# The third product of a two-element graph layer, by squared adjacency: seven block products with s3 held still

## The chip, the cores and the metric

The kernel runs on one core of a Trainium2 chip. The metric is the time of one execution on the device, in microseconds (us); the median of the runs counts. Five engines work side by side, each with its own queue in order: TensorE (PE; its weight loads PEld), VectorE (DVE), ScalarE (ACT), GpSimd (POOL) and SyncE (SP), which here only issues transfers. They wait for each other by semaphores that only count up.

## What is computed

Two graph networks follow one another, each with a residual and a layer norm. Only the first one, cut here, is touched by the change:

```python
def _slconv(x, adj, S, W):                       # S is adj: the weighting is adj squared
    support = jnp.einsum('bnf,fh->bnh', x, W)
    weighting = adj * S
    return jnp.einsum('nm,bmh->bnh', weighting, support)
h = jax.nn.relu(_slconv(x, adj, S, W1))          # W1 128 x 256
h = jax.nn.relu(_slconv(h, adj, S, W2))          # W2 256 x 512
return _slconv(h, adj, S, W3)                    # W3 512 x 128
...
x = _layernorm(x + _L0_gnn_ref(x, adj, adj, W1, W2, W3), axis=-1)   # x (8, 1024, 128), adj 1024 x 1024
x = _layernorm(x + _L1_gnn_ref(x, adj, ...), axis=-1)               # graph layers and four LSTMs
```

The third product of this text is the last one with the squared adjacency, adj^2 times s3, where s3 = h W3 is 1024 x 128 for each of the eight elements.

## The kernel before

Every float32 factor is kept as two parts, a high part that TensorE reads as it is and a low part that is the rest, so a product is three matmuls: high by high, high by low, low by high. ScalarE makes the high part (L1422, a copy with rounding), VectorE the low part (L1672, source less high part).

The eight elements go through the first network in **four pairs** ("pair" and `it`; elements 0 and 1 of a pair). Pair 0 is written out, pairs 1 and 2 are one loop body, the last pair is written out again. Then come the second network and its LSTMs in slots, which the change leaves as they are.

Products with the squared adjacency come in two forms. The products with x and with h1 use Strassen's scheme in Winograd's form: adj and the other factor are cut in 2 x 2 blocks of 512, and **seven block products** P1, P5, P6, P3, P7, P2, P4 take the place of eight. Each (`block_product`, L848) is twelve matmuls: four tiles of 128 columns of a block B held still, 512 columns of a block of adj or of its sums `sx` moving. The right-hand blocks are B11, B21, B22 and the differences T1 to T4; T1 = (B12's block, kept at T3) - B11, T2 = B22 - T1, T3 = B12 - B22, T4 = B21 - T2. Each is made as raw data (a copy from PSUM by ScalarE, or a subtraction by VectorE, L1822), then split. The results are added up by VectorE over q, r and the "C sums" (L1851, L1858, L1867).

The **third product** is done plainly. s3 of an element comes out of TensorE transposed (features on the partitions, `s3_product`). VectorE copies it to `s3t` (L1885), TensorE turns each half back by four transposes (`turn_half`, L1022), ScalarE and VectorE split it to `s3`. Then for each of eight rows of tiles m, four units u and two tiles t, a tile of adj is held still and 256 columns (both elements side by side) of s3 move: `a3_tile`, L1030, 8 x 4 x 2 x 3 = 192 matmuls of 256 columns. The result lies already as x does; VectorE adds it to x (`pair_sums`, L2063 and L2070), takes row statistics and, somewhat later, norms the rows.

While this runs, the next pair is made ready: GpSimd forms the differences of its x blocks (`x_diffs`, L794 to L799, four subtractions), ScalarE and VectorE split them as "n B11" to "n T4" to `t7`.

The order on each engine is written out by hand. The tables `MM_...`, `HI_...` and `LO_...` list the names that TensorE, ScalarE and VectorE signal, in order; a wait for a name is a wait for its place in the table. `BANK_OF` gives each result one of the eight PSUM banks. x is loaded to `xp` a first time for the differences and a second time, after "n T4", for the sums.

Of the kernel before, what the change touches and what calls it, by code (L numbers as in the profile page):

```python
# [38 lines left out]
def build(nc, x, adj_t, w1, w2, w3, wg0, bg0, wg1, bg1, wih_t, whh_t, bih, bhh, xn, out):  # L39
# [12 lines left out]
    with ctx:  # L52
# [46 lines left out]
        from_a11 = sb("from_a11", [P, 2, BANK], F32, s3t_at)  # L99
        tile_sum = sb("tile_sum", [P, N], F32, s3t_at + 4 * N)  # L100
# [138 lines left out]
        def w1_names(e, u0, u1):  # L239
# [3 lines left out]
        MM_TAIL = (h2_names(0, 0, 0, K3) + h2_names(0, 1, 0, 2) + ["0 s3 0"] + h2_names(0, 1, 2, K3)  # L243
                   + w1_names(1, 0, 2) + ["0 s3 1"] + w1_names(1, 2, 4)
                   + seven(1) + h2_names(1, 0, 0, K3) + h2_names(1, 1, 0, 2) + ["1 s3 0"] + h2_names(1, 1, 2, K3)
                   + ["turn 0 0", "turn 1 0", "1 s3 1", "turn 0 1", "turn 1 1", "a3 first"]
                   + [f"a3 {u}" for u in range(A3)])
        PLAIN = ["0 C11", "0 C12", "0 C21", "0 C22"]
        MM_FIRST = ["x0 0", "x0 1", "x1 0", "x1 1"] + w1_names(0, 0, 4) + PLAIN + MM_TAIL
        MM_NEXT = (["x P1", "x P5", "x P6", "x P3", "x P7", "x P2"] + w1_names(0, 0, 2) + ["x P4"]  # L250
                   + w1_names(0, 2, 4) + seven(0) + MM_TAIL)

# [4 lines left out]
        def hi_second(e, *names):  # L257
# [5 lines left out]
        HI_ONE = (["1 raw 0", "1 raw 1", "1 B11", "1 T1", "1 raw 2", "1 raw 3", "1 T2", "1 B22", "1 p1", "1 T4",  # L263
                   "1 T3", "1 B21"] + hi_second(1, *C_ORDER) + ["s3 0 0", "s3 1 0", "s3 0 1", "s3 1 1"])
        HI_X = ["n B11", "n B22", "n B21", "n T1", "n T2", "n T3", "n T4"]
        FROM_A11 = ["from a11 0", "from a11 1"]
        HI_TAIL = HI_ONE + HI_X + FROM_A11
# [5 lines left out]
        HI_LAST = HI_START + hi_second(0, *C_ORDER) + HI_ONE + ["n x"] + FROM_A11  # L273
# [4 lines left out]
        def lo_second(e, *names):  # L278
# [4 lines left out]
                   "1 T3", "1 B21", "1 T4", "1 r"] + lo_second(1, *LO_C) + ["s3 0 0", "s3 1 0", "1 s3t 1", "s3 0 1", "s3 1 1"])  # L283
        LO_X = ["n B11", "n B22", "n B21", "n T1", "n T2", "n T3", "n T4"]
        X_DIFFS = ("T1", "T2", "T3", "T4")
        LO_TAIL = LO_ONE + LO_X
# [5 lines left out]
        LO_START = SUMS + ["x q", "x r", "x C12 sum", "x C12", "x C22 sum", "x C22", "x C11", "0 T1 sum", "0 B11",  # L292
# [53 lines left out]
        def adj_part(i, m, cols):  # L346
            if cols is square_tile:
# [13 lines left out]

        def bank(name):
            return ps[:, BANK_OF[name], :]


        def c_block(e, name, part):

            n = {"C11": (0, 0), "C12": (1, 0), "C21": (0, 1), "C22": (1, 1)}[name]
            cols = slice(n[1] * BANK, (n[1] + 1) * BANK)
# [4 lines left out]
            return y2_raw[:, n[0], cols] if part == "raw" else y2[:, part, n[0], cols]  # L374

# [445 lines left out]
        def _(pe):  # L821
# [20 lines left out]
            B_BLOCK = {1: B11, 2: B21, 3: B22, 4: T4, 5: T1, 6: T2, 7: T3}  # L842

            def block_product(dst, v, start):
                for t in range(QUARTER):
                    tile = slice(t * P, (t + 1) * P)
                    for a, b in ((HI, HI), (HI, LO), (LO, HI)):
                        last = pe.matmul(dst, t7[:, B_BLOCK[v], a, tile], A_BLOCK[v](b, t),  # L848
# [85 lines left out]
            def pair_products(it):  # L934
                first = isinstance(it, int) and it == 0
# [49 lines left out]
                def adjacency(e):  # L985

                    lo_done(f"{e} B11")
                    signals(block_product(bank(f"{e} a"), 1, True), f"{e} P1")
                    lo_done(f"{e} T1")
                    signals(block_product(bank(f"{e} e"), 5, True), f"{e} P5")  # L990
                    lo_done(f"{e} T2")
                    signals(block_product(bank(f"{e} b"), 6, True), f"{e} P6")
                    lo_done(f"{e} B22")
                    signals(block_product(bank(f"{e} c"), 3, True), f"{e} P3")
                    lo_done(f"{e} r", f"{e} T3")
                    signals(block_product(bank(f"{e} b"), 7, False), f"{e} P7")
                    lo_done(f"{e} B21")
                    hi_done(f"{e} p1")
                    signals(block_product(bank(f"{e} a"), 2, False), f"{e} P2")
                    lo_done(f"{e} T4", f"{e} C22 sum")  # L1000
                    signals(block_product(bank(f"{e} b"), 4, False), f"{e} P4")
# [9 lines left out]
                def s3_product(e, half):  # L1011
# [4 lines left out]
                    signals(last, f"{e} s3 {half}")  # L1016

# [66 lines left out]
                turn_half(0, 0)  # L1084
                turn_half(1, 0)
                s3_product(1, 1)
                turn_half(0, 1)

                lo_done("s3 0 0", "s3 1 0")
                for m in range(MT):  # L1090
                    if m == 1:
                        turn_half(1, 1)
                    if m == QUARTER:
                        lo_done("s3 0 1", "s3 1 1")
                    for u in (2, 3, 0, 1) if m == QUARTER else range(A3):
                        if m == QUARTER and u < 2:
                            hi_done(f"from a11 {u}")
                        for t in range(2):
                            last = a3_tile(m, u, t)
# [1244 lines left out]
```

## Time and profile before

| | us |
|---|---|
| median of 3 runs | 983.54 |
| lowest, highest | 983.18, 983.77 |
| the profiled execution: its own time | 983.22 |
| its span on the core, in the profile | 981.5 |
| TensorE busy in the span | 966.2 (98%) |
| VectorE, ScalarE, GpSimd busy | 650.9, 429.9, 35.2 |
| one pair, start of the third product to the next one's | 120.42 |

The page of the profile gives, in this order, the busy time of each engine, the span in slices, the transfers, the chain of work that ended last and the costliest groups of instructions. Times of single rows are counted from the start of the span. The recorded time of a matmul runs to the end of its result, beyond the start of the next one; what a row of matmuls costs is the step from start to start. The same holds for VectorE and ScalarE, whose instructions overlap a little.

### The profile page before, as it was taken

To read this page: it belongs to the slowest core of one execution; us is meant where nothing else is said; L and a number is where in the kernel's file an instruction comes from. 1 tells how busy PE (TensorE), PEld (TensorE's weight loads), DVE (VectorE), ACT (ScalarE), POOL (GpSimd) and SP (SyncE) were. 2 spreads that over 40 slices of the span, in tenths; PEclk is the share of its full clock that TensorE was granted. 3 is DMA by queue.
4 is the path that set the end of the run, shared out by engine and by line. 5 is a ranking of instruction groups with operands and counts; after the bars stand their busy time and mean duration, and the time that the engine had idled before them with its cause. 6 is when DMAs were issued, how large, how long until landed. Compare 5 with 4: busy or idle time off the path is not lost.

```text
span 981.5 us, 14408 instructions
## 1 busy us (share of the span) xinstructions
PE 966.2 (98%) x5279; PEld 846.3 (86%) x5279; DVE 650.9 (66%) x1442; ACT 429.9 (44%) x788; POOL 35.2 (4%) x34
## 2 busy tenths in 40 slices
PE   9999999999999999999999999999999999999994
PEld 7888998889888898888988898898988889898894
DVE  7765557454575545754766656877776786877987
ACT  6353403433044331352434445455454555455765
POOL 0000200002000020000000001001010000100000
PEclk9999999999999999999999999999999999999998
DMA  8000000101011010104600000000000000000001
GB/s 306 1 1 1 13 32 18 69 1 44 0 43 43 0 43 1 61 26 143 232 2 0 1 1 1 0 2 22 1 1 22 0 22 0 22 1 22 1 1 65
DMA packets 11287, 31.01 MB, mean 32 GB/s; under 512 B 1120, under 2 KB 2400, under 8 KB 11232
## 3 DMA queue, kind: packets, MB, share of 16 engines
q1 hardware_dynamic: 11232, 30.30, 8.4%
q8 instruction: 32, 0.52, 0.2%
q14 instruction: 23, 0.19, 0.1%
HBM read 22.95 MB, written 7.34 MB: 31 GB/s over the span
## 4 chain that ended last, share of the span: by engine, by line
PE 95%; DVE 3%; ACT 1%; issue 1%; DVEq 0%; ACTq 0%
PE ps L1192 24%; PE ps L848 19%; PE ps L824 11%; PE ps L826 11%; PE ps L825 11%; PE ps L1030 9%; PE ps L1245 3%; PE ps L1265 2%; PE ps L866 2%; PE ps L1113 1%; PE ps L1022 1%; PE ps L1307 1%; DVE stats L1689 1%; PE ps L1339 1%; PE ps L1308 0%
## 5 line engine op out<-in xcount | busy, mean ns | idle before, releaser
L848 PE MATMUL ps<-adj,t 128*128 128x512 f32 x480 | 112.9, 390 | 0.0
L848 PEld LDWEIGHTS ps<-adj,t 128*128 128x128 f32 x480 | 89.3, 188 | 18.0
L1030 PE MATMUL ps<-s,adj 128*128 128x256 f32 x768 | 94.1, 284 | 0.0
L1030 PEld LDWEIGHTS ps<-s,adj 128*128 128x128 f32 x768 | 92.6, 192 | 0.0
L824 PE MATMUL ps<-adj,node 128*128 128x512 f32 x216 | 84.5, 391 | 0.1
L826 PE MATMUL ps<-adj,node 128*128 128x512 f32 x216 | 84.3, 390 | 0.0
L825 PE MATMUL ps<-adj,node 128*128 128x512 f32 x216 | 84.3, 390 | 0.0
L1610 ACT ACTIVATE gates_x<-ps,lb 128x258 f32<-128x258 f32 (+1 forms) x156 | 66.5, 508 | 40.3 <-PE ps L1192 40.2
L1610 ACT ACTIVATE gates<-ps,lb 128x512 f32<-128x512 f32 (+2 forms) x117 | 66.7, 647 | 37.9 <-PE ps L1192 28.7
L848 PE MATMUL ps<-sx,t 128*128 128x512 f32 x360 | 83.2, 389 | 0.0
L848 PEld LDWEIGHTS ps<-sx,t 128*128 128x128 f32 x360 | 67.6, 188 | 14.0
L1675 DVE SCALAR_TENSOR_TENSOR h<-ps,h 128x512 fp32r<-128x512 f32 x80 | 54.4, 688 | 37.2 <-ACT h L1422 37.2
L1192 PE MATMUL ps<-hw,lw 128*128 128x258 f32 (+1 forms) x468 | 72.4, 303 | 0.0
L1192 PEld LDWEIGHTS ps<-hw,lw 128*128 128x128 f32 x468 | 68.5, 190 | 2.3
L1422 ACT ACTIVATE y<-y_raw 128x512 fp32r<-128x512 f32 x27 | 17.1, 632 | 116.2 <-DVE y_raw L1867 116.2
L1422 ACT ACTIVATE h<-ps 128x512 fp32r<-128x512 f32 x64 | 38.1, 598 | 60.2 <-PE ps L826 60.2
L1192 PE MATMUL ps<-hstep_x,lw 128*128 128x258 f32 (+1 forms) x360 | 53.7, 298 | 0.0
L1192 PEld LDWEIGHTS ps<-hstep_x,lw 128*128 128x128 f32 x360 | 50.8, 189 | 0.4
L826 PE MATMUL ps<-y,w2s 128*128 128x512 f32 x128 | 49.8, 389 | 0.0
L824 PE MATMUL ps<-y,w2s 128*128 128x512 f32 x128 | 49.8, 389 | 0.0
L825 PE MATMUL ps<-y,w2s 128*128 128x512 f32 x128 | 49.8, 389 | 0.0
L826 PEld LDWEIGHTS ps<-adj,node 128*128 128x128 f32 x216 | 40.6, 188 | 8.5
(250 smaller groups left out, 1819.2 us busy)
## 6 DMA issues: line engine op xcount, KB each, us to landing
xb<-in_x SPq DMA_DIRECT2D x7, 1024.0 KB, 4.9
sx_raw<-in_adj_t SPq DMA_DIRECT2D x8, 512.0 KB, 8.6
adj_raw<-in_adj_t SPq DMA_DIRECT2D x8, 512.0 KB, 7.8
out<-xb SPq DMA_DIRECT2D x7, 512.0 KB, 2.6
xn<-xb SPq DMA_DIRECT2D x3, 1024.0 KB, 4.0
xb<-xn SPq DMA_DIRECT2D x6, 512.0 KB, 6.9
xb<-in_x SPq DMA_DIRECT2D x2, 512.0 KB, 5.4
lw_raw<-in_wih_t SPq DMA_DIRECT2D x1, 1024.0 KB, 11.3
```

Source lines behind the costliest of these rows:

```text
L824: pe.matmul(dst, stat(HI), mov(HI), start=start, stop=False)
L825: pe.matmul(dst, stat(HI), mov(LO), start=False, stop=False)
L826: return pe.matmul(dst, stat(LO), mov(HI), start=False, stop=stop)
L848: last = pe.matmul(dst, t7[:, B_BLOCK[v], a, tile], A_BLOCK[v](b, t), start=start and t == 0 and (a, b) == (HI, HI), stop=t == QUARTER - 1 ...
L866: pe.matmul(bank(f"{name} {half}"), of[:, a, m * P:(m + 1) * P], adj[:, b, m, half * BANK:(half + 1) * BANK], start=(m == 0 and (a, b) == ...
L1030: last = pe.matmul(dst, adj[:, a, m, nt:nt + P], s3[:, b, m, :, :].rearrange("p j c -> p (j c)"), start=(m == 0 and t == 0 and (a, b) == ( ...
L1192: done = pe.matmul(gate_bank(a), lw[:, i, weight, names[a] * F:(names[a] + 1) * F], state(j), start=start and (i, j) == (HI, HI), stop=sto ...
L1245: last = pe.matmul(mm_unit("adj_x", half), node[:, i, m * P:(m + 1) * P], adj[:, j, m, half * BANK:(half + 1) * BANK], start=(m == 0 and ( ...
L1265: last = pe.matmul(mm_unit("wg0", v)[:, t * F:(t + 1) * F], z[:, i, nt:nt + P], wgs[:, j, 0, :], start=(t == 0 and (i, j) == (HI, HI)), st ...
L1422: nc.scalar.activation(dst, src, func).then_inc(a_hi, 1)
L1610: nc.scalar.activation(gates_in(u.stream)[:, g, at], ps[:, (AHEAD["gate"][slot] + gate) % GB, 0:u.n], ACT.Tanh if g == GG else ACT.Sigmoid ...
L1675: nc.vector.scalar_tensor_tensor(out=dst, in0=src, scalar=0.0, in1=f32(hi), op0=ALU.max, op1=ALU.subtract).then_inc(done, 1)
```

## The change

In pairs 0, 1 and 2 the third product is done by seven block products as well; the last pair keeps the plain form.

- s3t of the two elements is turned back by `flip_half` (as `turn_half`, other banks): element 0's halves after the third block product of h1 of element 1 ("flip 0 0", "flip 0 1"), element 1's first half before "1 s3 1", its second half after P1 of the new stage. ScalarE copies each from PSUM as raw data (`flip_raw`); element 1 gives B11 and B21, element 0 gives B12 (at T3) and B22.
- The stage "s": T1 to T4 and the splits as in the other seven-block products, in tiles `s7_...` of their own laid over `node`, the place of y1, y2 and s3, and the end of the big buffer; then P1 (flip 1 1 behind it), P5, P6, P3, P7, P2, P4.
- The result is transposed (features on the partitions). Three of its blocks, C12, C22 and C11, are turned back at the end of the stage (`back_block`, 12 transposes), C21 after the first block product of the next pair (4 more). VectorE adds the four to x in four passes of 512 columns in place of six.
- The differences of the next x by GpSimd stay where they were, behind "1 s3 1"; "n B11" to "n T4" and r, the C sums of "s" are woven into one another on VectorE.

```diff
+        S3_AT = {"B22": node_at, "T3": node_at + 4 * KB, "B11": r2_at, "T1": r2_at + 4 * KB, "T2": r2_at + 8 * KB,
+                 "B21": r2_at + 12 * KB, "T4": big_at + 28 * KB}
...
+        MM_H2 = h2_names(1, 0, 0, K3) + h2_names(1, 1, 0, 2) + ["1 s3 0"] + h2_names(1, 1, 2, K3)
+        MM_TAIL = (MM_MIDDLE + seven(1)[:3] + ["flip 0 0", "flip 0 1"] + seven(1)[3:] + MM_H2
+                   + ["flip 1 0", "1 s3 1", "s P1", "flip 1 1"] + seven("s")[1:] + ["back C12", "back C22", "back C11"])
...
+        HI_TAIL = (HI_H1 + ["s raw 0 0", "s raw 0 1", "s B22"] + hi_second(1, *C_ORDER)
+                   + ["s raw 1 0", "s B11", "s T1", "s T2", "s T3", "s raw 1 1", "s p1", "s B21", "s T4", "n B11",
+                      "n B22", "n B21", "n T1", "n T2", "n T3", "n T4", "s C11"])
...
+        LO_TAIL = LO_ONE + ["s T1 sum", "s B11", "1 s3t 1", "s T2 sum", "s T1", "s T3 sum", "s B22", "s T4 sum", "s T2",
+                            "s T3", "s B21", "s q", "s T4", "n B11", "s r", "n B22", "n B21", "n T1", "n T2", "n T3",
+                            "n T4", "s C12 sum", "s C22 sum", "s C21 sum"]
...
+                def transposed(dst, src):
+                    for t in range(4):
+                        last = pe.transpose(dst[:, t * F:(t + 1) * F], src[:, t * P:(t + 1) * P], ident_f[:])
+                    return last
...
+                    pe.wait_ge(a_lo, reached_before("lo", it, "s C21 sum"))
+                    back_block("C21")
                     signals(block_product(bank("x e"), 5, True), "x P5")
...
+                else:
+                    flip_half(1, 0)
+                    s3_product(1, 1)
+                    adjacency("s")
+                    lo_done("s C12 sum")
+                    back_block("C12")
+                    lo_done("s C22 sum")
+                    back_block("C22")
+                    hi_done("s C11")
+                    back_block("C11")
...
+                    for name in BACK:
...
+                        nc.vector.tensor_tensor(rows, rows, bank(f"back {name}"), ALU.add).then_inc(a_lo, 1)
+                    own_done("sum C21")
                     row_stats(pair_rows(), stats_at(it - 1))
```

TensorE at the third product of pair 0, before (the twelve products on `h2` and `w3s` between the first two rows are left out):

```order
L1022 MATMUL ps<-ident_f_98,s3t_67 128x128 x4
L1030 MATMUL ps<-s3_63,adj_49 128x256 x24
L1022 MATMUL ps<-ident_f_98,s3t_67 128x128 x4
L1030 MATMUL ps<-s3_63,adj_49 128x256 x168
L1120 UNCONDITIONAL_BRANCH
```

and now:

```order
L874 MATMUL ps<-adj_49,s7_B11_73 128x512 x12
L1051 MATMUL ps<-ident_f_113,s3t_67 128x128 x4
L874 MATMUL ps<-sx_89,s7_T1_74 128x512 x12
L874 MATMUL ps<-sx_89,s7_T2_75 128x512 x12
L874 MATMUL ps<-sx_89,s7_B22_71 128x512 x12
L874 MATMUL ps<-adj_49,s7_T3_72 128x512 x12
L874 MATMUL ps<-adj_49,s7_B21_76 128x512 x12
L874 MATMUL ps<-adj_49,s7_T4_77 128x512 x12
L1051 MATMUL ps<-ident_f_113,a3_out_70 128x128 x12
```

The 192 products on adj held still have gone, and 84 of 512 columns with s3's blocks held still, then twelve transposes, stand there.

VectorE from the last two low parts of h2 of pair 0 on, before:

```order
L1675 SCALAR_TENSOR_TENSOR h2_54<-ps,h2_54 128x512 x2
L1672 TENSOR_TENSOR s3_63<-ps,s3_63 128x4x128 x2
L1885 COPY s3t_67<-ps 128x512
L1672 TENSOR_TENSOR s3_63<-ps,s3_63 128x4x128 x2
L1672 TENSOR_TENSOR t7_52<-xb_76,t7_52 128x512 x3
L1672 TENSOR_TENSOR t7_52<-t7_raw_53,t7_52 128x512 x4
```

and now:

```order
L1752 SCALAR_TENSOR_TENSOR h2_54<-ps,h2_54 128x512 x2
L1897 TENSOR_TENSOR s7_T1_raw_81<-s7_T3_raw_79,s7_B11_raw_80 128x512
L1749 TENSOR_TENSOR s7_B11_73<-s7_B11_raw_80,s7_B11_73 128x512
L1962 COPY s3t_67<-ps 128x512
L1897 TENSOR_TENSOR s7_T2_raw_82<-s7_B22_raw_78,s7_T1_raw_81 128x512
L1749 TENSOR_TENSOR s7_T1_74<-s7_T1_raw_81,s7_T1_74 128x512
L1897 TENSOR_TENSOR s7_T3_raw_79<-s7_T3_raw_79,s7_B22_raw_78 128x512
L1749 TENSOR_TENSOR s7_B22_71<-s7_B22_raw_78,s7_B22_71 128x512
L1897 TENSOR_TENSOR s7_T4_raw_84<-s7_B21_raw_83,s7_T2_raw_82 128x512
L1749 TENSOR_TENSOR s7_T2_75<-s7_T2_raw_82,s7_T2_75 128x512
```

Behind the copy of "1 s3 1" there stood one more split of s3 and then the next x; now there stand the differences and low parts of s3's blocks, each with two inputs in SBUF.

## Rows read from the trace of the kernel before

**Rows 1.** The page: busy time of the engines, and the chain by engine.

```profile
PE 966.2 (98%) x5279; PEld 846.3 (86%) x5279; DVE 650.9 (66%) x1442; ACT 429.9 (44%) x788; POOL 35.2 (4%) x34
...
PE 95%; DVE 3%; ACT 1%; issue 1%; DVEq 0%; ACTq 0%
```

**Rows 2.** Busy time by window; PEclk is the granted clock, last two are transfers.

```profile
core 0: us, PE busy (x) PEld busy (x) DVE busy (x) ACT busy (x) POOL busy (x), PEclk, DMA share, GB/s
110.87:231.29 120.42, 120.42 (x655) 104.77 (x654) 69.12 (x161) 38.59 (x66) 5.14 (x5) 1.00 0.08 27
...
106.90:134.41 27.51, 27.51 (x221) 26.98 (x220) 14.17 (x34) 7.50 (x14) 5.08 (x4) 1.00 0.12 39
```

**Rows 3.** Timeline of TensorE, pair 0 to 1: start, length, line, operation, count.

```profile
106.90 1.03 PE L1022 MATMUL ps<-ident_f,s3t 128*128 128x128 f32 x8
107.69 0.48 PE L824 MATMUL ps<-h,w3s 128*128 128x512 f32 x1
...
110.51 0.60 PE L1022 MATMUL ps<-ident_f,s3t 128*128 128x128 f32 x4
...
114.17 20.40 PE L1030 MATMUL ps<-s,adj 128*128 128x256 f32 x168
134.41 2.91 PE L848 MATMUL ps<-adj,t 128*128 128x512 f32 x12
137.16 8.32 PE L848 MATMUL ps<-sx,t 128*128 128x512 f32 x36
145.32 5.60 PE L848 MATMUL ps<-adj,t 128*128 128x512 f32 x24
150.76 0.28 PE L824 MATMUL ps<-w1s,y 128*128 128x256 f32 x1
```

**Rows 4.** Timeline of TensorE, transposes among 512-column products, in the later phase.

```profile
618.08 0.60 PE L1339 MATMUL ps<-ident_f,hfull 128*128 128x128 f32 x4
618.44 3.03 PE L1192 MATMUL ps<-hstep,lw 128*128 128x512 f32 x12
```

**Rows 5.** Timeline of ScalarE and VectorE at the third product of pair 0.

```profile
107.09 0.60 ACT L1422 ACTIVATE h<-ps 128x512 fp32r<-128x512 f32 x1 [0.77 <-PE ps L826]
...
107.72 0.69 DVE L1675 SCALAR_TENSOR_TENSOR h<-ps,h 128x512 fp32r<-128x512 f32 x1 [0.67 <-ACT h L1422]
...
110.71 0.69 DVE L1885 COPY s3t<-ps 128x512 f32<-128x512 f32 x1 [1.10 <-PE ps L826]
...
117.66 2.48 DVE L1672 TENSOR_TENSOR t<-t_raw,t 128x512 fp32r<-128x512 f32 x4
```

**Rows 6.** Timeline of GpSimd and of VectorE where they meet, pair 0.

```profile
110.83 1.29 POOL L794 TENSOR_TENSOR t_raw<-xb 128x512 f32<-128x512 f32 x1 [109.45 <-PE ps L826]
...
114.69 1.29 POOL L799 TENSOR_TENSOR t_raw<-xb,t_raw 128x512 f32<-128x512 f32 x1
...
115.70 0.83 DVE L1672 TENSOR_TENSOR t<-xb,t 128x512 fp32r<-128x512 f32 x1
```

**Rows 7.** Timeline of VectorE and of GpSimd near the end of the kernel.

```profile
914.89 0.72 DVE L2156 TENSOR_TENSOR gates_x<-gates_x 128x258 f32<-128x258 f32 x1
915.54 1.11 DVE L2158 TENSOR_TENSOR gates_x<-gates_x 128x258 f32<-128x258 f32 x1
916.68 0.43 DVE L2161 TENSOR_TENSOR gates_x<-gates_x 128x258 f32<-128x258 f32 x1
...
915.28 1.08 POOL L816 CAST hw_last<-ht_last 128x516 fp32r<-128x516 f32 x1
```

**Rows 8.** Timeline of TensorE, a restart after a wait for ScalarE.

```profile
958.72 0.96 PE L1317 MATMUL ps<-lw,wgs 128*128 128x512 f32 x3 [0.88 <-ACT gates_last L1610]
```

**Rows 9.** Timeline of VectorE: constants after pair 0, and the low part of C22.

```profile
120.09 0.06 DVE L2081 MEMSET sel<- 128x4 f32 x1
...
122.90 0.17 DVE L2100 MEMSET ones<- 128x128 f32 x1
...
149.62 0.69 DVE L1672 TENSOR_TENSOR y<-y_raw,y 128x512 fp32r<-128x512 f32 x1 [0.70 <-ACT y L1422]
```

More of the change, by code:

```diff
@@ L291, in build @@
         SUMS = ["sum a11 2", "sum a11 3", "sum 0", "sum 1", "sum 2", "sum 3"]
-        LO_START = SUMS + ["x q", "x r", "x C12 sum", "x C12", "x C22 sum", "x C22", "x C11", "0 T1 sum", "0 B11",
+        BACK = ("C12", "C22", "C11", "C21")
+        LO_START = [f"sum {name}" for name in BACK] + ["x q", "x r", "x C12 sum", "x C12", "x C22 sum", "x C22", "x C11", "0 T1 sum", "0 B11",
                            "x C21 sum", "0 T2 sum", "0 T1", "0 T4 sum", "0 T2", "0 T3 sum", "0 B22", "x C21", "0 q",
@@ L374, in c_block, with seven_block @@
             return y2_raw[:, n[0], cols] if part == "raw" else y2[:, part, n[0], cols]
+        BLOCK = {"B11": B11, "T1": T1, "T2": T2, "B22": B22, "T3": T3, "B21": B21, "T4": T4}
+        def seven_block(e, name, part):
+            if e == "s":
+                return s7_raw[name][:] if part == "raw" else s7[name][:, part, :]
+            return t7_raw[:, BLOCK[name], LO, :] if part == "raw" else t7[:, BLOCK[name], part, :]
         PLAIN_AT = {"C11": "a", "C12": "b", "C21": "e", "C22": "c"}
@@ L841, in _, with block_product @@
                        3: lambda i, t: sx[:, S4, i, t, :]}
-            B_BLOCK = {1: B11, 2: B21, 3: B22, 4: T4, 5: T1, 6: T2, 7: T3}
-            def block_product(dst, v, start):
+            B_BLOCK = {1: "B11", 2: "B21", 3: "B22", 4: "T4", 5: "T1", 6: "T2", 7: "T3"}
+            def block_product(dst, v, start, e=None):
                 for t in range(QUARTER):
@@ L1083, in pair_products @@
                 h2_product(1, 1, 3)
[L1084 to L1099, printed above, removed]
[L1100 to L1105 removed]
+                if last_pair:
+                    turn_half(0, 0)
+                    turn_half(1, 0)
+                    s3_product(1, 1)
+                    turn_half(0, 1)
+                    lo_done("s3 0 0", "s3 1 0")
+                    for m in range(MT):
+                        if m == 1:
+                            turn_half(1, 1)
+                        if m == QUARTER:
+                            lo_done("s3 0 1", "s3 1 1")
+                        for u in (2, 3, 0, 1) if m == QUARTER else range(A3):
+                            if m == QUARTER and u < 2:
+                                hi_done(f"from a11 {u}")
+                            for t in range(2):
+                                last = a3_tile(m, u, t)
+                            if (m, u) == (QUARTER - 1, 1):
+                                signals(last, "a3 first")
+                            if m == MT - 1:
+                                signals(last, f"a3 {u}")
+                        if m < MT - 1:
+                            last.then_inc(adj_used, 1)
+                else:
+                    flip_half(1, 0)
+                    s3_product(1, 1)
+                    adjacency("s")
[5 more added lines that the diff above has]
+                    back_block("C11")
@@ L1468, in turned_hi, with flip_raw @@
                           bank(f"turn {e} {half}").rearrange("p (t c) -> p t c", t=4), ACT.Copy)
+                def flip_raw(e, half):
+                    mm_done(f"flip {e} {half}")
+                    to = {(0, 0): "T3", (0, 1): "B22", (1, 0): "B11", (1, 1): "B21"}[e, half]
+                    hi_of(f"s raw {e} {half}", seven_block("s", to, "raw"), bank(f"flip {e} {half}"), ACT.Copy)
                 def x_hi_of(name):
@@ L1550, in pair @@
                 block_hi(1, "B21")
+                if not last_pair:
+                    flip_raw(0, 0)
+                    flip_raw(0, 1)
+                    block_hi("s", "B22")
                 c_hi(1, "C12")
@@ L1570, in pair @@
                         block_hi("n", name)
-                if last_pair:
+                    mm_done("s P2")
+                    hi_of("s C11", c_block("s", "C11", "raw"), bank("s a"), ACT.Copy)
+                else:
+                    turned_hi(0, 0)
+                    turned_hi(1, 0)
+                    turned_hi(0, 1)
+                    turned_hi(1, 1)
                     act.wait_ge(xb_in, 16 * (B - 2))
@@ L1575, in pair @@
                     tile_hi(1)
-                for u in range(2):
-                    mm_done("a3 first")
-                    hi_of(f"from a11 {u}", from_a11[:, u, :], bank(f"a3 {u}"), ACT.Copy)
+                    for u in range(2):
+                        mm_done("a3 first")
+                        hi_of(f"from a11 {u}", from_a11[:, u, :], bank(f"a3 {u}"), ACT.Copy)
                 assert n_hi[0] == len(names)
```

171 lines of the change are left out of this document (102 added, 69 removed), and 2 rows, old and new, of the table BANK_OF.

## The prediction, on record before the changed kernel was timed

> **What bounds the kernel now.** I read the page's shares first: TensorE is busy in 98% of the span and the chain that ended last lies on it for 95% [rows 1]. So a microsecond taken off TensorE's queue is one microsecond of time, as long as nobody makes TensorE wait. The table by windows then gives the frame of the phase that is changed: one pair takes 120.42 us, TensorE is busy in all of it, and the granted clock is 1.00 [rows 2]. The changed stretch of a pair goes from the first transpose of the third layer to the next pair's first block product, 106.90 to 134.41, 27.51 us, with VectorE at half load and GpSimd busy for 5.08 us in it [rows 2, 3]. This is why the second thing to read is who else could become late: today the others have slack here, and the change takes it away.
>
> **TensorE, what goes.** In those 27.51 us lie the twelve s3 products, which are unchanged. Their step is that of every 512-column product: 36 of them from 137.16 to 145.32, so 226.7 ns each, 2.72 us for twelve [rows 3]. The rest, 27.51 - 2.72 = 24.79 us, is the 192 products of 256 columns and four groups of transposes (8, 4 and 4 instructions in three places). For the big part of it: 168 products in 114.17 to 134.41, 120.5 ns each, against 226.7 ns for twice the columns. So a 256-column product costs more than half of a 512-column one, and the old stage is 192 such.
>
> **What comes.** Seven block products of twelve, 84 x 226.7 ns = 19.04 us; same form of stationary and moving operand as the ones timed. Then 32 transposes instead of 16. Among 512-column products a transpose costs more than its own step: eight start at 106.90 and the next product at 107.69, and from there to the transpose at 110.51 twelve products take 2.82 instead of 2.72, so eight cost 0.79 + 0.10 = 0.89 [rows 3]. Four: 618.08 to 618.44 is 0.36; the next twelve products end after 3.03, where 11 steps and a last one of 0.39 (the 36 above take 8.32, 0.16 beyond their steps) are 2.88, so 0.51 in all [rows 4]; as eight lose only 0.10 behind them, I take 0.49. Twelve, at 0.11 each from the same rows: 1.36. The change has groups of 8, 4, 4, 12 and 4: 0.89 + 3 x 0.49 + 1.36 = 3.72 us. TensorE's work thus goes from 24.79 to 19.04 + 3.72 = 22.76: **2.03 us less per pair**, 6.1 us in three pairs. Bounds: 2.7 if a group costs only its 0.09 to 0.11 steps, 1.7 if every group costs 0.1 more. The last pair keeps the old form and the phase after the pairs is untouched.
>
> **Who makes TensorE wait.** Now every block product needs a B block or a difference of B blocks, each split in a high part (ScalarE) and a low part (VectorE), all made from s3 while the stage is already running. I walk it in the clock of pair 0, 0.89 later than before since eight transposes now stand in the product before. Durations and hand-over: a ScalarE pass over 512 columns 0.60, a VectorE one 0.69, or 0.60 for each more in a row; a pass starts 0.03 after what it waits for (107.69 to 107.72) [rows 5].
> P1 could start at 111.00: flip at 107.79, 0.49, 2.72. B11: raw copy to 109.08, high to 109.71, low to 110.42. In time by 0.6.
> P5 could start at 111.00 + 2.72 + 0.49 = 114.21 and needs T1's low part, P6 2.72 later and needs T2's. VectorE cannot begin these before it has copied "1 s3 1" (result there at 111.16, copy 111.19 to 111.88), because its queue is in order. Undisturbed: T2 sum to 112.5, T1 low to 113.1, T3 sum to 113.7, B22 low to 114.3, T4 sum after the copy of flip 1 1 by ScalarE at about 115.0, so to 115.7, T2 low to 116.3. P5 and P6 would be in time by 1.1 and 0.6 us, and the whole 2.03 us would stay.
>
> **The disturbance.** GpSimd makes its four differences of x, 1.29 us each, exactly then: it waits for the same "1 s3 1" as VectorE's copy and starts right behind it, 110.83 after 110.71 [rows 5, 6]. Before, VectorE had at that time a copy from PSUM, 0.69 long with GpSimd running beside it [rows 5], and little else. The one VectorE pass with two SBUF inputs that still met GpSimd's last difference is the one at 115.70: 0.83 instead of 0.68, ended at 116.53, 0.55 after GpSimd's 115.98 [rows 6]. So it did not run beside it: it waited until 0.13 before GpSimd's end and then took its 0.68. And in 914.89 to 916.65 the two take turns: a VectorE product ends at 915.61, the next was issued at 915.54 right behind it but takes 1.11 us where the following one takes 0.43, because a GpSimd cast, issued at 915.28 and ended at 916.36, came in between; again VectorE ends 0.29 after it, 0.14 before and 0.43 of its own [rows 7].
> The Trainium skill says the same: "SBUF — State Buffer", section "Who interferes with whom", has a VectorE instruction with two SBUF inputs and a GpSimd instruction that reads SBUF exclude each other, the later one to issue blocked until the other is done; by that rule, which the rows above bear out, the stage is paced by both engines together and not by the slower one.
> T2 sum, T1 low, T3 sum, B22 low, T4 sum and T2 low all have two SBUF inputs. Taking turns: GpSimd 1 starts some 0.1 behind the copy, 111.26 to 112.55; T2 sum ends 112.55 + 0.55 = 113.10. GpSimd 2 gets in just before that (I take the same 0.12 the other way round), ends 114.27; T1 low ends 114.82. GpSimd 3 to 115.99; T3 sum ends 116.54. GpSimd 4 to 117.71; B22 low ends 118.26, T4 sum 118.86, T2 low 119.46. ScalarE's copy of flip 1 1 stands behind T3's high part in its queue (117.2) and is there at 117.8, just before T4 sum wants it. A restart costs TensorE the hand-over and an exposed weight load: three products took 0.96 after a wait, where 2 x 0.227 + 0.39 is 0.84, so 0.12 [rows 8]. P5 starts at 114.82 + 0.15 = 114.97 instead of 114.21, wait 0.76; P6 could start at 117.69 and starts at 119.61, wait 1.92. **2.68 us of waits per pair.** From there VectorE is free of GpSimd and catches up: r is ready at about 123.2 and P7 starts at 125.05; the sum that P4 needs is there about 1.5 us before it.
>
> **The start of the next pair.** The four sums, the row statistics and q, r come about as late against the block products as before, so pairs 2 and 3 wait for nothing. In pair 1 VectorE's constants (120.09 to 123.07), which lay in idle time, now lie between the last sum of pair 0 and the first of pair 1. Low C22, ended at 150.31 for a product at 150.76 before [rows 9], has by the same walk between 0 and 0.2 left: I put 0.1 us, once.
>
> **Sum.** 3 x (2.68 - 2.03) + 0.1 = +2.05 us. Against the profiled execution: span 981.5 to 983.6. It lies 1.7 us of start and end below its own time of 983.22, which is 0.3 below the median 983.54; the difference is put on the median: 983.54 + 2.05 = **985.6 us**. The likeliest case's own range is 983.8 to 987.6: 0.35 us per pair either way on the transposes and 0.5 on the waits.
>
> **Rivals.**
> (a) VectorE keeps its turn. If a waiting GpSimd gets in only where VectorE's queue has a gap, T1 low ends at 113.7 and P5 is in time; the gap comes at 115, before T4 sum, and T2 low ends at 117.2: wait 0.5 us per pair. 3 x (0.5 - 2.03) + 0.1 = -4.5: 979.0 us. This is the case on the other side. It speaks for it that VectorE's passes stand back to back here; against it the turn at 915.54, where a pass issued right behind the last one was overtaken [rows 7]. It decides at one row: the second and third GpSimd difference of the stage longer than 1.29 us by several VectorE passes.
> (b) No exclusion at all: no wait, 3 x -2.03 + 0.1 = -6.0: 977.5. Against it stands the 0.83 [rows 6].
> (c) The turns hold but one of the two waits is smaller, since GpSimd starts later or T1 low slips in before its second: 1 us less per pair, 982.6.
> (d) Worse: ScalarE's copy of flip 1 1 comes late for T4 sum (it has some 0.4 us), or T2 low loses one more turn: 1 us more per pair, 988.6.
> That the products of the stage are not as fast as the others' is the rival in which the change does not do what it says; nothing in the profile speaks for it, and it is in the bounds above.
>
> **Chances.** Likeliest case 0.68, (a) 0.10, (b) 0.05, (c) 0.08, (d) 0.09. A measurement of this kernel can tell about 0.2%, 1.97 us, from no change: under 981.6 is faster, over 985.5 slower. The likeliest case lies on that border: I give 0.36 of its 0.68 to slower and 0.32 to the same; with (d) slower is 0.44, with half of (c) the same is 0.36, and faster is (a), (b), the other half of (c) and a rest: 0.20. The range goes from (a) to nearly (d): 978.8 to 988.5, and leaves out (b), part of (a) and part of (d), some 0.15.
>
> **What the profile after would show.** Products on blocks of s3: step 0.227 us. A group of four transposes among them: under 0.5 us. TensorE idle before the weight load of the second and the third product of the stage, released by VectorE's low part of T1 and of T2, about 0.8 and 1.9 us, in all three pairs, and nowhere else. VectorE's differences and low parts there about 1.3 us long beside GpSimd and 0.68 after it; GpSimd's four differences stretched over 6.5 us instead of 5.15. Pair to pair 121.1 us instead of 120.4. The forecast is wrong if TensorE has no idle time there (b), if GpSimd is stretched to much over 7 us (a), or if TensorE waits at a third place, above all P7 for r.

## The result, and the profile after

The changed kernel takes **985.38 us** (median; 984.93 to 985.97), the kernel before 983.25 us in the same comparison (983.1 to 983.77). The ratio is 1.0021, with a 95% interval of 1.0012 to 1.003: slower by 2.13 us, where +2.05 was forecast. The profiled execution's own time is 984.93 us, its span 983.1, so the two traces that are compared here lie 1.6 to 1.7 us apart.

The page of the kernel after, busy time by engine and the chain by engine; the rows before are [rows 1]:

```profile
PE 961.5 (98%) x5003; PEld 828.1 (84%) x5003; DVE 679.4 (69%) x1472; ACT 442.8 (45%) x809; POOL 38.9 (4%) x34
...
PE 92%; DVE 5%; issue 1%; ACT 1%; DVEq 0%; ACTq 0%
```

TensorE has less to do (961.5 instead of 966.2 us busy), and yet the kernel is longer. VectorE's share of the chain has gone from 3% to 5%: work of VectorE now stands between two products. GpSimd's busy time has grown from 35.2 to 38.9 us although its 34 instructions are the old ones. Which VectorE work that is, the table of TensorE's waits tells (line waited at, releaser, then total us, times, longest). In the kernel before no line of that table named a block of s3:

```profile
PEld ps L874 <- DVE s_T L1749: 8.4, 6, 2.0
```

Six waits, two in each of three pairs. The timeline of TensorE in pair 0 of the kernel after shows where they lie; these rows answer to [rows 3] (start, length, line, form, count, and in brackets the idle time before it and who ended it):

```profile
110.35 2.88 PE L874 MATMUL ps<-adj,s_B 128*128 128x512 f32 x12
113.07 0.60 PE L1051 MATMUL ps<-ident_f,s3t 128*128 128x128 f32 x4
114.26 3.01 PE L874 MATMUL ps<-sx,s_T 128*128 128x512 f32 x12 [0.59 <-DVE s_T L1749]
118.86 3.06 PE L874 MATMUL ps<-sx,s_T 128*128 128x512 f32 x12 [1.59 <-DVE s_T L1749]
121.75 2.88 PE L874 MATMUL ps<-sx,s_B 128*128 128x512 f32 x12
124.47 2.88 PE L874 MATMUL ps<-adj,s_T 128*128 128x512 f32 x12
...
132.64 1.47 PE L1051 MATMUL ps<-ident_f,a_out 128*128 128x128 f32 x12
133.87 3.02 PE L874 MATMUL ps<-adj,t 128*128 128x512 f32 x12
```

The two rows of `sx,s_T` are P5 and P6, on T1 and T2 of s3. From the starts: with the flip at its 0.49, P5 could have come at 110.35 + 2.72 + 0.49 = 113.56 and comes at 114.26, 0.70 late; P6 could have come at 114.26 + 2.72 = 116.98 and comes at 118.86, 1.88 late, and the product behind it comes after 2.89 instead of 2.72, 0.17 for the restart. From there on the steps are 2.72. From the first column of P1 to the transposes back is 132.64 - 110.35 = 22.29 us: seven times 2.72, 0.49 for the flip, and 2.76 for the waits (0.70 + 1.88 + 0.17, rounded). Pairs 1 and 2 read the same way with slightly smaller waits: P5 starts 0.62 late, P6 1.89 late, and the restart costs 0.13, in all 2.64 and 2.65 us.

VectorE and then GpSimd at the same place (GpSimd's rows answer to [rows 6]):

```profile
110.55 0.69 DVE L1962 COPY s3t<-ps 128x512 f32<-128x512 f32 x1 [0.69 <-PE ps L852]
111.16 1.35 DVE L1897 TENSOR_TENSOR s_T_raw<-s_B_raw,s_T_raw 128x512 f32<-128x512 f32 x1
112.43 1.77 DVE L1749 TENSOR_TENSOR s_T<-s_T_raw,s_T 128x512 fp32r<-128x512 f32 x1
114.12 1.77 DVE L1897 TENSOR_TENSOR s_T_raw<-s_T_raw,s_B_raw 128x512 f32<-128x512 f32 x1
115.82 1.78 DVE L1749 TENSOR_TENSOR s_B<-s_B_raw,s_B 128x512 fp32r<-128x512 f32 x1
117.53 0.68 DVE L1897 TENSOR_TENSOR s_T_raw<-s_B_raw,s_T_raw 128x512 f32<-128x512 f32 x1
118.13 1.28 DVE L1749 TENSOR_TENSOR s_T<-s_T_raw,s_T 128x512 fp32r<-128x512 f32 x2
```

```profile
110.67 1.29 POOL L820 TENSOR_TENSOR t_raw<-xb 128x512 f32<-128x512 f32 x1 [109.28 <-PE ps L852]
112.03 1.62 POOL L822 TENSOR_TENSOR t_raw<-xb,t_raw 128x512 f32<-128x512 f32 x1
113.61 1.73 POOL L823 TENSOR_TENSOR t_raw<-xb 128x512 f32<-128x512 f32 x1
115.31 1.74 POOL L825 TENSOR_TENSOR t_raw<-xb,t_raw 128x512 f32<-128x512 f32 x1
```

Read the two listings as one sequence in which the engines alternate. VectorE's rows are, in order, the copy, T2's sum, T1 low, T3's sum, B22 low, T4's sum and T2 low (with T3 low in the last row). T2's sum ends at 112.51, 0.55 after GpSimd's 111.96; T1 low at 114.20, 0.55 after 113.65; T3's sum at 115.89, 0.55 after 115.34; B22 low at 117.60, 0.55 after 117.05. Each GpSimd pass in its turn ends 1.14 to 1.16 after the VectorE pass ahead of it. Pairs 1 and 2 show the same four meetings each, with 0.54 to 0.55. As soon as GpSimd is through, VectorE is back at 0.68. T1 low ends at 114.20 and P5 starts at 114.26; T2 low ends near 118.8 and P6 starts at 118.86.

### The profile page after: what moved, and what is told of

Read it like the earlier page. It is cut to its first block, busy times and chain, and to the rows that moved or that the text cites. A ratio compares the mean times of both kernels' runs of the same rounds, so it can differ in the third digit from the quotient of the medians.

```text
span 983.1 us, 13960 instructions
## 1 busy us (share of the span) xinstructions
PE 961.5 (98%) x5003; PEld 828.1 (84%) x5003; DVE 679.4 (69%) x1472; ACT 442.8 (45%) x809; POOL 38.9 (4%) x34
## 4 chain that ended last, share of the span: by engine, by line
PE 92%; DVE 5%; issue 1%; ACT 1%; DVEq 0%; ACTq 0%
PE ps L874 24%; PE ps L1249 24%; PE ps L850 11%; PE ps L851 11%; PE ps L852 11%; PE ps L1302 3%; PE ps L1074 2%; PE ps L1322 2%; PE ps L892 2%; DVE s_T_raw L1897 1%; PE ps L1051 1%; PE ps L1364 1%; PE ps L1170 1%; DVE stats L1766 1%; DVE s_T L1749 1%
## 5 line engine op out<-in xcount | busy, mean ns | idle before, releaser
L852 PEld LDWEIGHTS ps<-adj,node 128*128 128x128 f32 x216 | 40.5, 188 | 8.5
L850 PEld LDWEIGHTS ps<-adj,node 128*128 128x128 f32 x216 | 40.6, 188 | 8.3 <-DVE node L1752 0.5
L851 PEld LDWEIGHTS ps<-adj,node 128*128 128x128 f32 x216 | 40.6, 188 | 7.8
```

What stands on the lines that cost most here:

```text
L850: pe.matmul(dst, stat(HI), mov(HI), start=start, stop=False)
L851: pe.matmul(dst, stat(HI), mov(LO), start=False, stop=False)
L852: return pe.matmul(dst, stat(LO), mov(HI), start=False, stop=stop)
```

## Experiments

The theory has two halves. **One:** the new form is worth 2.03 us of TensorE per pair, and nothing else in the kernel is slower for it. **Two:** those 2.03 us are eaten by two waits that come from VectorE and GpSimd taking turns (a VectorE pass and a GpSimd pass that meet run one after the other), so that it matters only which VectorE rows stand in the contested stretch. Rivals: the waits are a matter of the new products or transposes; or of the amount of VectorE work, whatever GpSimd does. Seven kernels ran; all ratios are against runs of the kernel before on the same chip (983.3 us). A second yardstick is the distance from the flip in the middle of the stage (the four transposes at 113.07 above) to the same flip of the next pair: 120.42 us in the kernel before.

### Another order on VectorE, all work kept

```
-  "s B11", "1 s3t 1", "s T2 sum", "s T1", "s T3 sum", "s B22", "s T4 sum", "s T2", "s T3", ... "n B11", "s r",
+  "s B11", "s T2 sum", "s T1", "1 s3t 1", "s T2", "s T3 sum", "s B22", "s T4 sum", "s T3", ... "s r", "n B11",
   (T2 low is now written before T4's sum reads T2's raw block, so that
    raw block moves to a half of the raw tile of x that is unused here)
+                if (name, part) == ("T2", "raw"):
+                    return t7_raw[:, T3, HI, :]
```

> From the changed kernel, VectorE's rows in the squared-adj stage in another order: the sum of T2's parts, T1 low and T2 low come ahead of or right behind the copy of s3's second block and ahead of the sum of T3's parts and B22 low, and r comes ahead of the n blocks. All the work stays, GpSimd's four x differences too. Theory (the turns with GpSimd make T1 low and T2 low late for P5 and P6, and nothing else does): both waits go, though VectorE's passes beside GpSimd stay long (about 1.7 us instead of 1.3) and GpSimd's four still spread over more than 6 us. The stage between the first column of P1 and the 12 transposes takes 19.04 + 0.49 = 19.5 us, 2.03 less per pair than before less nothing: 983.25 - 3 x 2.03 + 0.1 = 977.3 us, range 976.5 to 978.8. Rival 1 (the waits belong to something else, for example to the products or the transposes of the new place): about 985. Rival 2 (the turns only move to another row: T3 low, T4 low or q becomes late for P7 or the transposes): a wait of 0.5 to 1 us per pair remains at another product, 979 to 980.5.

Measured: **977.21 us** (976.95 to 977.86), ratio 0.9938 (0.9924 to 0.9952). Flip to flip: 118.35 us in both intervals, 2.07 less than before. TensorE's timeline of pair 0:

```profile
111.19 2.89 PE L876 MATMUL ps<-adj,s_B 128*128 128x512 f32 x12
113.91 0.60 PE L1053 MATMUL ps<-ident_f,s3t 128*128 128x128 f32 x4
114.27 5.74 PE L876 MATMUL ps<-sx,s_T 128*128 128x512 f32 x24
...
130.72 1.47 PE L1053 MATMUL ps<-ident_f,a_out 128*128 128x128 f32 x12
```

P5 and P6 are now one row of 24 without idle time, and the stage is 130.72 - 111.19 = 19.53 us: 7 x 2.72 + 0.49. VectorE there (the second row is T1 low, the third the copy, the fourth T2 low) and GpSimd's first pass:

```profile
110.64 0.68 DVE L1899 TENSOR_TENSOR t_raw<-s_B_raw,s_T_raw 128x512 f32<-128x512 f32 x1
111.24 0.69 DVE L1751 TENSOR_TENSOR s_T<-s_T_raw,s_T 128x512 fp32r<-128x512 f32 x1
111.84 0.68 DVE L1964 COPY s3t<-ps 128x512 f32<-128x512 f32 x1
112.44 1.18 DVE L1751 TENSOR_TENSOR s_T<-t_raw,s_T 128x512 fp32r<-128x512 f32 x1
113.54 1.76 DVE L1899 TENSOR_TENSOR s_T_raw<-s_T_raw,s_B_raw 128x512 f32<-128x512 f32 x1
```

```profile
111.51 1.57 POOL L822 TENSOR_TENSOR t_raw<-xb 128x512 f32<-128x512 f32 x1 [110.12 <-PE ps L854]
```

The turns are still there: the rows from 113.54 on are 1.76 to 1.78 long, as in the changed kernel. But T1 low is through at 111.93 and T2 low at 113.62, before P5 (114.27) and P6 need them. So both halves hold: same engines, same work, same collision, and the time falls by 8.17 us against the changed kernel. The saving against the kernel before is 6.10 us in three pairs, 2.03 each, as in the sum (the distances from flip to flip, in the trace, give 2.07). This version beats both kernels.

### GpSimd writes only

```
-  nc.gpsimd.tensor_tensor(raw(T1), x_block("B12"), x_block("B11"), ALU.subtract).then_inc(x_diff, 1)
+  nc.gpsimd.tensor_tensor(spare[:, 0:1], x_block("B12")[:, 0:1], x_block("B11")[:, 0:1], ALU.subtract)
+  nc.gpsimd.memset(raw(T1), 0.5).then_inc(x_diff, 1)
   (and so for T2, T3, T4)
```

> From the changed kernel, GpSimd's four x differences replaced by fills of the same four blocks, which write 512 values a partition and read none; a subtraction of one column on a spare tile stays ahead of each. So the differences of the next x are left out of the computation. VectorE's order is that of the changed kernel. Theory (the two engines exclude each other while both read SBUF with two inputs): no VectorE pass beside the fills is longer than 1.35 us, P5 and P6 do not wait: 983.25 - 3 x 2.03 + 0.1 = 977.3 us, range 976.5 to 978.8. Rival (any work of GpSimd on SBUF, a write too, holds VectorE up): passes stay at 1.7, the waits stay at 0.8 and 1.9, 985.

Measured: 977.18 us (976.95 to 977.37), ratio 0.9938 (0.9923 to 0.9953); flip to flip 118.34. VectorE's order is the changed kernel's, and only GpSimd's work is another. Its first rows, T2's sum and T1 low on VectorE, and below them GpSimd:

```profile
111.18 0.69 DVE L1902 TENSOR_TENSOR s_T_raw<-s_B_raw,s_T_raw 128x512 f32<-128x512 f32 x1
111.78 0.69 DVE L1754 TENSOR_TENSOR s_T<-s_T_raw,s_T 128x512 fp32r<-128x512 f32 x1
```

```profile
110.81 0.53 POOL L822 MEMSET t_raw<- 128x512 f32 x1
111.42 0.49 POOL L824 TENSOR_TENSOR spare<-xb 128x1 f32<-128x1 f32 x1
...
112.33 0.19 POOL L826 TENSOR_TENSOR spare<-xb 128x1 f32<-128x1 f32 x1
```

VectorE's passes are 0.69 long right across the fills. The only instruction that shows a hold is GpSimd's subtraction of one column at 111.42, 0.49 instead of 0.19: it reads SBUF, and it ends at 111.91 when T2's sum ends at 111.87. So no product or transpose of the new stage is to blame, nor VectorE's load: with the old order and the turns gone, the full saving is there. The fills are also shorter than the differences (0.53 us instead of 1.29), so this run alone does not separate reading from length; the next one does, with copies of nearly the fills' length that do read.

### GpSimd copies: one input

```
-  nc.gpsimd.memset(raw(T1), 0.5).then_inc(x_diff, 1)
+  nc.gpsimd.tensor_copy(raw(T1), x_block("B12")).then_inc(x_diff, 1)
   (against the kernel of the previous experiment; and so for T2, T3, T4)
```

> From the changed kernel, GpSimd's four x differences replaced by copies of one x block each (one input of 512 values a partition from SBUF, the same four outputs); a subtraction of one column on a spare tile stays ahead of each. So the differences of the next x are left out of the computation. VectorE's order is that of the changed kernel. Theory A (the two engines exclude each other only while GpSimd's instruction has two inputs in SBUF): no VectorE pass beside the copies is longer than 0.7 us, no waits, 977.3 us. Theory B (any read of SBUF by GpSimd is enough): VectorE's passes beside the copies are stretched to a copy's length plus about 0.55 us, and waits of P5 and P6 remain; with copies of 0.7 to 1.3 us, 979 to 985.

Measured: 978.64 us (978.34 to 979.02), ratio 0.9952 (0.9936 to 0.9969), 0.4 below the low end of theory B. T2's and T3's sum on VectorE, then GpSimd:

```profile
111.49 0.80 DVE L1902 TENSOR_TENSOR s_T_raw<-s_B_raw,s_T_raw 128x512 f32<-128x512 f32 x1
...
112.81 1.10 DVE L1902 TENSOR_TENSOR s_T_raw<-s_T_raw,s_B_raw 128x512 f32<-128x512 f32 x1
```

```profile
111.13 0.61 POOL L822 COPY t_raw<-xb 128x512 f32<-128x512 f32 x1
111.82 0.52 POOL L824 TENSOR_TENSOR spare<-xb 128x1 f32<-128x1 f32 x1
112.28 1.08 POOL L825 COPY t_raw<-xb 128x512 f32<-128x512 f32 x1
```

The copy at 111.13 ends at 111.74 and T2's sum at 112.29, 0.55 later; the copy at 112.28 ends at 113.36 and T3's sum at 113.91, again 0.55 later. One input on GpSimd's side is enough, so theory A falls: what counts is that GpSimd reads SBUF at all. The sizes are smaller, as a copy takes 0.61 us where it is not held and a difference 1.29. One wait is left, P6 for T2 low, 1.5 us in three pairs, and the time is 1.5 us above that of the fills. The Trainium skill has both results in one sentence of "SBUF — State Buffer", section "Who interferes with whom": a VectorE instruction with two SBUF inputs contends with a GpSimd instruction that reads SBUF, not with one that only writes it. Both runs agree with it (0.80 and 1.10 us beside copies, 0.69 beside fills).

### Every difference twice

```
+  nc.gpsimd.tensor_tensor(t7_raw[:, T1, HI, :], x_block("B12"), x_block("B11"), ALU.subtract)
   nc.gpsimd.tensor_tensor(raw(T1), x_block("B12"), x_block("B11"), ALU.subtract).then_inc(x_diff, 1)
   (and so for T2, T3, T4)
```

> From the changed kernel, each of GpSimd's four x differences is done twice (eight passes; the first of each pair goes to an unused half of the raw tile). Theory (strict turns: as long as GpSimd has a pass to run, VectorE's next pass with two inputs from SBUF waits for its end): the sum of T4's parts and T2 low each lose a turn of about 1.1 us too, the wait of P6 for T2 low grows from 1.9 to about 4.1 us and that of P5 stays at 0.8: 985.4 + 3 x 2.2 = 992 us, range 990 to 994. Rival (no turns; VectorE is held up only by a fixed number of passes after GpSimd starts, or by GpSimd's first passes): the waits stay as they are, 985.4. Rival 2 (VectorE keeps the ports once it has them): 985 to 986.

Measured: 996.93 us (996.01 to 998.0), ratio 1.0137 (1.0121 to 1.0152). The waits are what the theory of strict turns said; the rest was not foreseen. TensorE's waits, and P5 and P6 in pairs 0 and 1:

```profile
PEld ps L878 <- DVE s_T L1753: 14.8, 6, 4.2
```

```profile
114.70 3.04 PE L878 MATMUL ps<-sx,s_T 128*128 128x512 f32 x12 [0.58 <-DVE s_T L1753]
121.45 4.47 PE L878 MATMUL ps<-sx,s_T 128*128 128x512 f32 x12 [3.71 <-DVE s_T L1753]
...
246.17 5.49 PE L878 MATMUL ps<-sx,s_T 128*128 128x512 f32 x12 [3.73 <-DVE s_T L1753]
```

All eight GpSimd passes but the first are 1.62 to 1.74 long and VectorE's passes from T1 low to B21 low, seven in a row, are 1.7 to 1.8: the turns go on as long as GpSimd has work. P5's wait has not changed (0.58 idle instead of 0.59); P6's is 4.2 instead of 2.0, the 2.2 more of the expectation. 8.4 + 3 x 2.2 = 15.0 us of waits were expected and 14.8 came, so 992. The missing 4.9 us (5.6 in the profiled execution, which took 997.6) are in the lengths: P6's twelve products take 4.47 us in pair 0, 5.49 in pair 1 and 4.43 in pair 2, instead of the 3.06, 3.02 and 3.01 of the changed kernel, 5.3 us in all. The windows of pair 1 tell why (the seventh figure is the granted clock, 1.00 being 2.4 GHz):

```profile
244.00:246.00 2.00, 0.00 (x0) 0.00 (x0) 2.00 (x2) 1.52 (x3) 2.00 (x2) 0.89 0.00 0
246.00:248.00 2.00, 1.83 (x4) 1.50 (x5) 2.00 (x3) 2.00 (x5) 2.00 (x2) 0.50 0.00 0
```

In pair 1 the clock begins to fall in the course of the 3.7 us idle time (0.89 in the first window) and reads 0.50, 1.2 GHz, from 246 to 252, where P6 runs; in pair 0 it still reads 1.00 when P6 starts at 121.45 and 0.50 from 123 on. In this trace P6 alone pays 1.4 us (pairs 0 and 2) and 2.5 us (pair 1) for it, on top of the wait.

### GpSimd later

```
   pool.wait_ge(a_mm, reached("mm", it, "1 s3 1"))
+  pool.wait_ge(a_lo, reached("lo", it, "s r"))
   nc.gpsimd.tensor_tensor(raw(T1), x_block("B12"), x_block("B11"), ALU.subtract).then_inc(x_diff, 1)
```

> From the changed kernel, GpSimd's four x differences start only when VectorE has done r, the last row that this stage's products need. Theory: T1 low and T2 low come in time, P5 and P6 do not wait; the differences now lie beside the n passes and the C sums, so the n rows of T1 to T4 come later and the C22 sum queued behind them on VectorE is late for the product that reuses its bank: 0.5 to 1.5 us per pair there. 983.25 - 3 x 2.03 + 0.1 + 3 x 1.0 = 980.3 us, range 977.5 to 982. It also shows whether a VectorE pass with one input in PSUM (the C sums, 0.69 us alone) is held up beside GpSimd. Rival (the waits of P5 and P6 are no matter of GpSimd): they stay, and with the new one the time is 988.

Measured: 989.34 us (988.52 to 990.14), ratio 1.0064 (1.0049 to 1.0079), 9 us above what was expected and outside its range. The waits of P5 and P6 are gone, as the theory says, and a dearer one has come, at P4, the last product of the stage, for the sum of C22 that empties its bank. The table of waits, P4 in pairs 0 and 1, then the rows of VectorE that it waits for:

```profile
PEld ps L875 <- DVE a_out L1945: 8.1, 3, 2.8
```

```profile
130.31 3.02 PE L875 MATMUL ps<-adj,s_T 128*128 128x512 f32 x12 [2.14 <-DVE a_out L1945]
...
251.28 4.61 PE L875 MATMUL ps<-adj,s_T 128*128 128x512 f32 x12 [2.33 <-DVE a_out L1945]
```

```profile
124.21 1.76 DVE L1750 TENSOR_TENSOR t<-t_raw,t 128x512 fp32r<-128x512 f32 x1 [1.18 <-POOL t_raw L823]
127.16 1.90 DVE L1750 TENSOR_TENSOR t<-t_raw,t 128x512 fp32r<-128x512 f32 x3 [1.18 <-POOL t_raw L826]
128.97 1.28 DVE L1945 TENSOR_TENSOR a_out<-ps,a_out 128x512 f32<-128x512 f32 x2
```

The expectation had named the queue but priced only the longer passes. The low parts of the next x also need GpSimd's results: VectorE stands still for 1.18 us twice, with the C22 sum queued behind it. That makes 2.7 per pair instead of 1.0. And again the clock: in pair 0 it stays at 1.00 after the 2.14 us, in pairs 1 and 2 P4's twelve products take 4.61 and 4.56 us instead of 3.02. One window of pair 1:

```profile
252.00:254.00 2.00, 2.00 (x7) 1.58 (x6) 0.00 (x0) 0.00 (x0) 0.00 (x0) 0.53 0.99 406
```

The sum is 977.2 + 8.1 + 2 x 1.6 = 988.5, and the profiled execution, from which its terms are read, took 988.55. The median is 0.8 higher because two of the four executions took 990.1; no trace of those is kept, so what they paid for stays open. Whether the C sums, which have one input in PSUM and one in SBUF, run undisturbed beside GpSimd this run doesn't show, as none met a GpSimd pass in it. The trace of the kernel before has a pass of that kind, the low part of s3, beside the GpSimd difference of 114.69 to 115.98 in [rows 6]:

```profile
115.08 0.69 DVE L1672 TENSOR_TENSOR s<-ps,s 128x512 fp32r<-128x512 f32 x1 [2.61 <-ACT s L1422]
```

Neither is stretched, 0.69 and 1.29, and the same holds for the pass at 111.78, which overlaps the first two differences. So it is the passes with both inputs in SBUF that are held, and not VectorE's two-input passes as such.

### Half of the reordering

```
-  "s B11", "s T2 sum", "s T1", "1 s3t 1", "s T2", "s T3 sum", ...
+  "s B11", "1 s3t 1", "s T2 sum", "s T1", "s T2", "s T3 sum", ...
   (against the first experiment's kernel)
```

> Half of the reordering: VectorE's copy of s3's second block stands first again, as in the changed kernel, but T2 low is written right behind T1 low, ahead of the sum of T3's parts, and r ahead of the n blocks. Theory (each wait is a row's place in the turns, and the two waits add up since each pushes TensorE once): P5 waits 0.83 us for T1 low as in the changed kernel, P6 doesn't wait: 977.2 + 3 x 0.83 = 979.7 us. Rival (the waits don't add up; the first one's push is hidden behind the second, or the second's goes to P7 for B22 low): 983 to 985.

Measured: 980.27 us (979.85 to 980.56), ratio 0.9968 (0.9955 to 0.998).

```profile
114.80 5.74 PE L876 MATMUL ps<-sx,s_T 128*128 128x512 f32 x24 [0.59 <-DVE s_T L1751]
...
123.10 3.00 PE L876 MATMUL ps<-adj,s_T 128*128 128x512 f32 x12
```

P5 waits as in the changed kernel, 0.59 us of idle time by the row (0.70 late, and 0.14 more in the 5.58 us that P5 and P6 take; P3 starts at 120.38), and P6 follows without a gap. That is the 0.83 of the expectation. The waits add up: with P6's gone, what is left is P5's. The remaining 0.6 us over the 979.7 goes with a third, small wait that came with this order, of P7's weight load for r (L1937 is the sum r). The table of waits, and r in pair 0:

```profile
PEld ps L876 <- DVE a_out L1937: 0.8, 3, 0.3
```

```profile
122.34 0.69 DVE L1937 TENSOR_TENSOR a_out<-ps,a_out 128x512 f32<-128x512 f32 x1
```

r ends at 123.03 and P7 starts at 123.10. It is late because T4's sum, five rows ahead of it on VectorE, started 0.58 us after VectorE was free, when ScalarE had copied flip 1 1; ScalarE in its turn had waited until 118.17 for T3's sum, which this order moves behind T2 low. P7 for r is the third place that the prediction had named as the likeliest; the changed kernel doesn't wait there, this order does.

### The kernel before, with fills

```
-  nc.gpsimd.tensor_tensor(raw(T1), x_block("B12"), x_block("B11"), ALU.subtract).then_inc(x_diff, 1)
+  nc.gpsimd.tensor_tensor(spare[:, 0:1], x_block("B12")[:, 0:1], x_block("B11")[:, 0:1], ALU.subtract)
+  nc.gpsimd.memset(raw(T1), 0.5).then_inc(x_diff, 1)
   (on the kernel before; and so for T2, T3, T4)
```

> From the kernel before (third product by 256 columns), GpSimd's four x differences replaced by the fills that write only; the differences of the next x are left out. Theory (in the kernel before the same turns are taken, but every row that a product needs is ready with room to spare): VectorE's passes there shorten to 0.69 us and the time stays 983.3, within 0.5 us. Rival (the turns cost the kernel before something too, through VectorE or ScalarE work that isn't in TensorE's waits): 1 us or more faster.

Measured: 983.30 us (983.1 to 983.77), ratio 1.0 (0.999 to 1.0009); flip to flip 120.42, as before. The collision of [rows 6] is gone (the row `115.53 1.90 ... x3` instead of 2.04 for the same three passes) and the time has not moved. So the turns cost the kernel before nothing; the change is what put TensorE behind them.

## Why the prediction was right

By its own steps:

- **TensorE's work.** Forecast 22.76 us in place of 24.79. The stage without waits is 19.53 us from P1 to the transposes back, as in the sum (19.04 + 0.49); the twelve transposes cost 1.23 + 0.14 = 1.37 (132.64 to 133.87, and 3.02 instead of 2.88 for the products behind), forecast 1.36. Flip to flip the saving is 2.07 us in the two runs without waits, forecast 2.03. Two small slips in its working change nothing: twelve transposes at 0.11 are 1.32 and not 1.36, and the lower bound, five groups at 0.1 more each, is 1.5 and not 1.7.
- **The walk of the blocks.** T1 low and T2 low were named as the two that come late. Forecast waits 0.76 and 1.92; read 0.70 and 1.88 in pair 0, 0.62 and 1.89 in pairs 1 and 2. The restart behind P6 cost 0.13 to 0.17 more, which the sum had not put there. In all 2.76, 2.64 and 2.65 instead of 2.68.
- **The turns.** Forecast: the VectorE pass that meets a GpSimd difference ends 0.55 behind it, and the next difference gets in before the next pass. All four differences of each of the three pairs do so. In detail the VectorE passes are 1.77 long rather than the "about 1.3" under what the profile would show: such a row holds the whole turn, 0.08 of overlap with the row before, 1.14 to 1.16 to the end of GpSimd's pass and 0.55 behind it. The instants in the walk were right, that one description of them was not. GpSimd's four take 6.38 us, forecast 6.5.
- **No third wait.** P7 starts at 124.47 for r, straight behind its forerunner, and P4's C sum is in time. Pair to pair was forecast at 121.1 and is 121.10 and 120.99.
- **The constants, +0.1 once.** Not seen. C22's low part in pair 1 is done at 149.66 + 0.69 = 150.35 and the product at 150.79 starts without idle time. This term was not needed; its room was 0.44 us where the prediction saw at most 0.2.
- **Rivals.** (a), VectorE keeps its turn, and (b), no exclusion, are refuted by the alternation in the two timelines and by the doubled differences, where eight VectorE passes in a row (T2's sum with 1.35 us, seven with 1.7 to 1.8) were held, one by each of GpSimd's eight. (b)'s number, 977.5, is the time that the fills gave, 977.18: it is what the kernel costs when the exclusion is removed. (c) and (d) did not occur: both waits were there in full, and ScalarE's copy of flip 1 1, done at 117.05, was in time for T4's sum, which started at 117.53, straight behind B22 low. In the doubled differences T4's sum and T2 low did lose their turns, which is (d)'s mechanism, with the size it should have.
- **How the sum hit.** With what was read, waits of 2.76 + 2.64 + 2.65 = 8.05 us and a saving of 3 x 2.07 = 6.2 give +1.8 us; the two traces differ by 1.6 in span and 1.7 in time, the medians by 2.13. Waits and saving were each right to 0.1 us per pair, so the mechanism and both sizes are shown. That the medians' +2.13 lies within 0.1 of the forecast +2.05 is closer than the terms warrant, and in part luck: the +0.1 did not happen, and some 0.3 us of the median's rise is in no row followed here.
- **Which side of the border.** The prediction split its chances at 981.6 and 985.5 us. 985.38 lies 0.12 below the upper one, in "the same" (0.36 of the chances) and not in "slower" (0.44). But those borders were drawn around 983.54, and the kernel before took 983.25 in this comparison; against that the rise is 2.13 us, and the interval of the ratio, 1.0012 to 1.003, lies wholly above 1.

What stays open is how the hand-over decides between a waiting GpSimd and a VectorE pass that is already queued. In the timelines read here GpSimd got in each time; why it did, no run tests.

## What to carry to other kernels

When a change shortens the busiest engine's stage by building more of its operands on others, walk each new operand to the product that wants it, and look for a second engine that shares something with the one that builds it: here 2 us per pair were won on TensorE and 2.7 lost to two operands queued behind work that could wait. Where the loss is a matter of turns, as here, order can mend it without less work: put what a product waits for ahead of the contested stretch, and let what has room to spare take the stretched passes. Moving the other engine instead (the later GpSimd) moved the wait here to what was queued behind its results, and made it dearer. A new order has to be walked as well: half of the reordering made a small new wait at P7.

## What the hardware showed that I had not expected

- **A wait can cost more than its length.** After idle times of 3.7 us (doubled differences) TensorE's granted clock went to 0.50 (1.2 GHz) and the next twelve products took 4.47, 5.49 and 4.43 us instead of 3.01 to 3.06; after 2.33 us it did so in two pairs of the later GpSimd (4.61 and 4.56 us, windows down to 0.53 and 0.50), while after 2.14 us in pair 0 of that kernel, and after the 1.59 us of the changed kernel, the products took 3.02 and 3.06. In the changed kernel the waits cost no clock.
- **A GpSimd instruction of one column is held too.** It took 0.19 us alone and 0.49 to 0.63 us where a VectorE pass with two SBUF inputs was under way.
- **A VectorE copy from PSUM is not held.** It took 0.68 us at 111.84 in the first experiment, inside a GpSimd difference that ran from 111.51 to 113.08, while the passes with two SBUF inputs beside it took 1.2 to 1.8. Nor was a pass with one input in PSUM and one in SBUF, 0.69 us at 115.08 in the kernel before.
